# Eight-stage graph and mixture-of-experts kernel: no dummy transposes ahead of six stages

## The reference

```
x = x + L0_gnn(norm(x))    # similarity of nodes, 5 rounds of propagation
x = x + L0_ffn(norm(x))    # 8 experts, 512 -> 1024 -> 512, gelu, top 2
x = x + L1_gnn(norm(x))    # aggregate, two 512x512 products, norm
x = x + L1_ffn(norm(x))    # router layer: 8 experts with 32 hidden units, top 1
x = x + L2_gnn(norm(x))    # 4 experts, 2 layers, two 512x512 products per layer
x = x + L2_ffn(norm(x))    # 8 experts, 512 -> 2048 -> 512, weighed by a tree of gates
x = x + L3_gnn(norm(x))    # attention over edges, norm, small FFN, norm
x = x + L3_ffn(norm(x))    # shared expert and 8 experts, 512 -> 1024 -> 512, silu
```

## Time and profile before

| | |
|---|---|
| median of 3 executions | 560.28 us |
| profiled execution | 560.0 us |
| its span, first to last instruction | 558.2 us |
| outside the span | 1.8 us |
| TensorE matmuls busy | 543.2 us |
| VectorE busy | 499.1 us |
| ScalarE busy | 425.4 us |
| GpSimd busy | 102.2 us |
| dummy transposes (L741) | 227, 28.5 us busy |

### The profile page before, as it was taken

One profiled execution on the slowest core, in us unless ns is written; L12 is line 12 of the kernel. 1 busy time (PEld: TensorE's weight loads), 2 busy tenths in 40 slices (PEclk: granted clock), 3 DMA queues, 4 the chain that ended last, 5 costly groups with the idle time before them and its releaser, 6 DMA issues.

```text
span 558.2 us, 8559 instructions
## 1 busy us (share of the span) xinstructions
PE 543.2 (97%) x2815; PEld 450.9 (81%) x2815; DVE 499.1 (89%) x485; ACT 425.4 (76%) x441; POOL 102.2 (18%) x69
## 2 busy tenths in 40 slices
PE   7999999999899999999999999999989999999998
PEld 7787888888688887788888888888968878888887
DVE  5799999988778878999999999999987889989996
ACT  5687888874287878788888888888845288788783
POOL 2044341000000003344344354310000100000000
PEclk9999999999999999999999999999999999999999
DMA  7989999995268885889999999999990369999910
GB/s 299 386 326 424 418 375 366 343 336 230 80 231 330 316 318 237 310 313 360 351 360 350 359 361 333 365 362 341 330 381 17 124 268 382 361 353 359 352 60 19
DMA packets 27545, 170.06 MB, mean 305 GB/s; under 512 B 4777, under 2 KB 5162, under 8 KB 7547
## 3 DMA queue, kind: packets, MB, share of 16 engines
q1 hardware_dynamic: 25986, 166.72, 78.1%
q10 hardware_dynamic: 1536, 3.04, 2.1%
HBM read 169.49 MB, written 0.26 MB: 304 GB/s over the span
## 4 chain that ended last, share of the span: by engine, by line
PE 74%; issue 12%; DVE 7%; ACT 2%; POOL 1%; DVEq 0%; POOLq 0%
PE pre L701 32%; PE y L701 29%; PE tp L727 5%; DVE w_lo L1149 2%; PE pre L719 2%; PE y L719 2%; PE wt L741 2%; ACT w_hi L414 1%; DVE w_lo L1156 1%; POOL rstd L358 1%; PE ms L754 0%; PE tp L734 0%; PE wt L764 0%; PE pre L1036 0%; PE pre L923 0%
## 5 line engine op out<-in xcount | busy, mean ns | idle before, releaser
L1149 DVE TENSOR_TENSOR w_lo<-raw,w_hi 128x2048 fp32r<-128x2048 f32 x146 | 342.6, 2374 | 24.9 <-ACT w_hi L414 23.9
L414 ACT ACTIVATE w_hi<-raw 128x2048 fp32r<-128x2048 f32 x152 | 287.9, 1917 | 0.6 <-issue 0.6
L487 ACT ACTIVATE hT_hi<-tp 128x512 fp32r<-128x512 f32 x66 | 39.5, 598 | 54.1 <-PE tp L727 54.0
L701 PE MATMUL pre<-w_hi,x_hi 128*128 128x512 f32 x292 | 79.3, 393 | 1.2 <-ACT x_hi L427 1.1
L701 PE MATMUL pre<-w_hi,x_lo 128*128 128x512 f32 x292 | 78.4, 390 | 0.5 <-DVE x_lo L1125 0.5
L701 PE MATMUL pre<-w_lo,x_hi 128*128 128x512 f32 x292 | 78.5, 391 | 0.0
L701 PE MATMUL y<-w_hi,hT_hi 128*128 128x512 f32 x256 | 74.9, 414 | 0.0
L701 PE MATMUL y<-w_lo,hT_hi 128*128 128x512 f32 x256 | 69.2, 392 | 0.0
L701 PE MATMUL y<-w_hi,hT_lo 128*128 128x512 f32 x256 | 68.7, 390 | 0.0
L701 PEld LDWEIGHTS pre<-w_hi,x_hi 128*128 128x128 f32 x292 | 54.0, 188 | 14.6 <-issue 3.0
L701 PEld LDWEIGHTS pre<-w_hi,x_lo 128*128 128x128 f32 x292 | 54.7, 188 | 12.4 <-DVE x_lo L1125 0.9
(11 more groups left out here) (314 smaller groups left out, 508.2 us busy)
## 6 DMA issues: line engine op xcount, KB each, us to landing
raw<-in_chunks SPq DMA_DIRECT2D x156, 1024.0 KB, 5.1
bias_wide<-in_L_ffn_b SPq DMA_DIRECT2D x4, 256.0 KB, 11.7
bias_wide<-in_L_ffn_b ACTq DMA_DIRECT2D x4, 256.0 KB, 6.3
side<-in_L_gnn_emb ACTq DMA_DIRECT2D x1, 512.0 KB, 6.3
affine<-in_L_ffn_W SPq DMA_DIRECT2D x1, 512.0 KB, 6.3
side<-in_L_ffn_W SPq DMA_DIRECT2D x1, 512.0 KB, 10.6
affine<-in_L_gnn_ln_g ACTq DMA_DIRECT2D x2, 256.0 KB, 6.2
affine<-in_L_gnn_ln_b ACTq DMA_DIRECT2D x2, 256.0 KB, 9.5
```

Of the source, the lines that this page charges most:

```text
L414: act.activation(w_hi[:, g % SPLIT_SLOTS], raw[:, g % RAW_SLOTS], ACT.Copy).then_inc(w_hi_ready, 4)
L487: act.activation(hT_hi[:, (s - 1) % 2], tp[:].rearrange("p (c n) -> p c n", n=P), ACT.Copy).then_inc(hT_hi_ready, 1)
L701: last = pe.matmul(dst, xs[:, k], ws[:, k], start=start and i == 0, stop=stop and i == len(passes) - 1, skip_group_check=seeded)
L1149: dve.tensor_tensor(w_lo[:, i], raw[:, g % RAW_SLOTS], w_hi[:, i].bitcast(F32), ALU.subtract).then_inc(w_lo_ready, 4)
```

## The change

Six entries of a table become zero: l0f 11, l1g 12, l2g 19, l2f 30, l3g 13, l3f 7. That is 92 of the 227 dummy transposes. l1f keeps its 35, and the groups with counts of their own stay.

```diff
-BRIDGE = {"l0g": 0, "l0f": 11, "l1g": 12, "l1f": 35, "l2g": 19, "l2f": 30, "l3g": 13, "l3f": 7}
+BRIDGE = {"l0g": 0, "l0f": 0, "l1g": 0, "l1f": 35, "l2g": 0, "l2f": 0, "l3g": 0, "l3f": 0}
```

## The result

| | before | after |
|---|---|---|
| median | 560.1 us (5 executions) | 562.95 us (5 executions) |
| lowest to highest | 559.43 to 560.37 | 561.4 to 565.84 |
| profiled execution, its span | 560.0, 558.2 | 561.4, 559.7 |
| mean granted clock of the profiled execution | 1.000 | 0.988 |

The ratio is 1.0058, 95% interval 1.0033 to 1.0083: slower by 2.9 us by the medians, by 0.6% by the ratio. The profiled execution is the fastest of its five.

A forecast was written before the change was run, and what follows sets the result against it. It took TensorE, busy for 97% of the span, to bound the kernel. 1.0 us freed against 1.5 falls of 1.5 us gave +1.25 us, 561.25 for the profiled execution and a median of 561.5; range 558.9 to 564.4.

The forecast's parts named there:

- the likeliest case: The clock falls at one or both long pauses, l2g and l2f: 560.8 or 562.3 us, chance 0.42.
- What is freed: Late dummies gone, the turn starts earlier: 0.25 us at l1g and 0.75 at l3f, together 1.0 (0.8 to 1.1).
- Where TensorE waits anyway: At l0f, l2g, l2f and l3g TensorE waits for `XN` behind the dummies, so removing them frees 0 us.
- How many falls: Clock falls at l2f and l2g, not at both in every execution: 1.5 falls as the middle.
- The price of a fall: Time lost when the clock drops to 1.2 GHz behind a pause: 1.5 us a fall, bounds 0 and 3.8.
- The bound of 3.8: Upper bound in us for one fall, if the clock stays down as long as at the start (8.1 x 0.47).
- The sum: Freed time and falls added over the kernel: -1.0 + 1.5 x 1.5 = +1.25 us.
- The rival with three or four falls: Clock falls at l3g too, or at four places: +3.5 to +5.0 us, 563.8 to 565.3, chance 0.18.
- The rule beside it: The skill page's rule that waits between matmul bursts bring back half rate; taken as speaking against this change, no size given.

The follow-up runs named there:

- l1g_full_rows: Kernel before without l1g's 12 dummies, its one-row bias matmuls replaced by 128-row identity matmuls (biases left out of the result); 559.11 us, ratio 0.9981.
- l1g9_l3f0: Kernel before with 9 dummies instead of 12 ahead of l1g and none instead of 7 ahead of l3f; 558.25 us, ratio 0.9965.
- l1g_only: Kernel before with only the 12 dummies ahead of l1g taken out; 559.85 us, ratio 0.9992.
- half: Kernel before with dummies cut to l0f 0, l1g 6, l2g 10, l2f 15, l3g 6, l3f 0; 561.88 us, ratio 1.0039.
- l2g_only: Kernel before with only the 19 dummies ahead of l2g taken out; 559.79 us, ratio 1.0007.
- after_again: The changed kernel itself, measured once more in a later comparison against the kernel before; 563.85 us, ratio 1.0078.

## Why the prediction was right or wrong

It forecast 561.5, slower by 1.25, with falls of the clock as the reason; it came to be slower by 2.85, for that reason. The median lies in the range, but above the likeliest case's own (560.5 to 562.6); the case that came, four falls, had been given 0.18. The steps:

- *What is freed.* Right. l3f gave 0.76 in the profile after (0.75 predicted). l1g gave 0.15 to 0.2 where 0.25 was predicted: with the clock up, L885 to the transpose at L910 is 10.06 us in l1g_full_rows (there L912) and 10.02 in l1g9_l3f0 instead of 10.21. Its turn starts 0.55 us after `XN` in the profile after (124.62 to 125.17) and 0.46 in l1g9_l3f0 (126.56 to 127.02), where the prediction took 0.47 from l0f.
- *Where TensorE waits anyway.* Right: at l0f, l2g, l2f and l3g the turn stands as far behind the last product as before, with pauses of 1.65, 3.4, 3.8 and 2.4 us.
- *How many falls.* Here the prediction failed: 1.5 were put in the sum, the profile has four, and executions have up to seven times the loss of one. Two steps were wrong. l3g's pause was set aside as short; it fell in 12 of 12. And l1g was taken as nearly shown harmless, because a pause of 1.31 us at l2g had left the clock up. That compared idle times alone. At l2g dense dummies stood ahead of the 1.31 us, at l1g matmuls on one row, which the profile counts as busy and behind which the clock fell (l1g_only against l1g_full_rows; in half even with 0.17 us of idle time).
- *The price of a fall.* 1.5 was too high on the mean, though not at l2g. In the profile after it is 0.7 to 1.6, 1.0 on the mean of the four stages. At l2g the delay behind the turn grows to 1.59 us and stays. At l3g it grows to 1.43 up to the last matmul ahead of the one that waited for `x_lo`, is 0.87 at that one and 0.76 behind it; at l2f it grows to 1.22 and is 0.73 behind the next turn of `h` (L727). These stages have waits of their own, which the slower matmuls fill; the prediction named waits of 0.2 and 0.48 us, and took only 0.2 off its 1.7. The bound of 3.8 was needed: the executions of l2g_only with a fall are some 3 us longer.
- *The sum.* 1.5 falls at 1.5 us are 2.25; four at about 1.0 are 4.1. Too few and too dear, the two errors took part of each other away; that the range held is in part luck. The rival with three or four falls was right in kind and 0.9 to 2.4 us too high.
- *The rule beside it.* The Trainium skill, page "TensorE: Matmul & The Clock Gate", section "HAM oscillation — how this bites in real kernels", has waits between bursts bring the clock to half rate. The runs agree at l2f and l3g (24 of 24 executions) and only in part at l2g (5 of 12); at l0f, 1.65 us of waiting in 11 executions did nothing.

## What to carry to other kernels

Don't judge a pause of TensorE by its idle time alone: here 3.38 us often did nothing, and 0.17 us behind six dummies and a stretch of one-row matmuls went with a fall. Look at what runs ahead of the pause, and at the granted clock of the stretch behind it, not of the pause: idle time on a seam costs nothing there, and half speed in the next stage does. If a pause is filled, fill it to its end, since with half of the dummies the clock still fell in 12 of 12 executions; but never past it, because a dummy that is still queued when the operand is ready is paid in full (seven at l3f, 0.76 us). Time such a change over many executions with their clocks, since the same pause may fall in one and not in the next.

## What the runs showed of the hardware

- Six one-row matmuls, over 1.8 us (124.58 to 126.42 in l1g_only), ahead of 1.07 us of idle time went with a fall in 12 of 12 executions; identity matmuls with 128 rows of the same widths ahead of 1.06 us in none of 12. With six dummies behind the one-row matmuls and 0.17 us of idle time the profile of half has a fall there too; with nine and no idle time the profile of l1g9_l3f0 has none.
- Where no wait takes it up, a fall of one short stretch costs 1.6 us (l2g in after, after_again and half); with waits of the stage behind it, 0.7 to 1.0 (l2f, l3g).
- A pause of 3.38 us at l2g left the clock up in 7 of 12 executions, while one of 2.4 us at l3g let it fall in 12 of 12. The first is followed by dense work; behind the second stand two more short waits in the profile before, of 0.30 us for `x_hi` and 0.48 for `x_lo`. That these make the difference was not tried.
- The start of an execution differs by up to 2.3 us (L877 begins at 18.8 to 21.1 us), more than any of the six edits, each alone, moved the median.
